# Attention denominators from GpSimd's sums of three P chunks, with the main and the dca denominator in one accumulation

## The reference, cut to what matters

```
y_dca  = y[:, -16:, :] ;  y_main = y[:, :-16, :]
q = LN(x @ Wq + bq) per head ;  k, v from y_main ;  k_dca, v_dca from y_dca
ctx     = softmax(q k^T * SCALE) v              # over 496 main rows
ctx_dca = softmax(q k_dca^T * SCALE) v_dca      # over 16 dca rows
x = x + (ctx + ctx_dca) @ Wo + bo
x = x + moe_ffn(layernorm(x))                   # 7 routed experts, top 2, and a shared one
```

## Time and profile before

| | us |
|---|---|
| median of three runs | 1215.59 |
| the profiled execution | 1215.54 |
| its span | 1213.4 |
| attention, first score matmul to last GpSimd instruction | about 188.0 to 512.3 |
| one group of four heads, in the middle of attention | 18.67 |

### The profile page before, as it was taken

The page is one execution under the profiler, slowest core; times in us unless marked ns, Lnnn a source line. Parts: engine busy times, 40 slices in busy tenths (PEclk is TensorE's granted clock), DMA queues, the critical chain, the costliest instruction groups (busy, mean ns, idle before and its releaser), DMA issues. The chain is left out here.

```text
span 1213.4 us, 18924 instructions
## 1 busy us (share of the span) xinstructions
PE 1050.7 (87%) x5825; PEld 478.9 (39%) x5826; DVE 631.5 (52%) x1123; ACT 491.9 (41%) x886; POOL 558.6 (46%) x505
## 2 busy tenths in 40 slices
PE   2789955999999999689439999999999999967896
PEld 1445431222222222145315545445545455523453
DVE  6777744677777777445543333233333322215644
ACT  2466553566666666323213333333333333312231
POOL 1365551143434421232337799898999800032111
PEclk9889985899999999889759999999999999989899
DMA  6144451222122211045136434333434311146244
GB/s 233 40 116 127 135 143 52 58 77 76 61 80 62 76 62 42 19 160 180 72 119 245 165 124 137 121 121 121 138 122 137 104 52 52 35 146 228 87 122 139
DMA packets 88074, 133.02 MB, mean 110 GB/s; under 512 B 7992, under 2 KB 46904, under 8 KB 88016
## 3 DMA queue, kind: packets, MB, share of 16 engines
q1 hardware_dynamic: 75040, 90.55, 23.5%
q0 software_dynamic: 11648, 40.38, 9.8%
q10 hardware_dynamic: 1328, 1.36, 0.4%
HBM read 85.60 MB, written 46.66 MB: 109 GB/s over the span
## 5 line engine op out<-in xcount | busy, mean ns | idle before, releaser
L866 DVE TENSOR_REDUCE nm<-a_psS 128x2 bf16<-128x992 f32 x128 | 152.8, 1194 | 83.9 <-PE a_psS L877 83.9
L807 ACT ACTIVATE p_t<-a_psT 128x512 f32<-128x512 f32 x256 | 145.6, 595 | 62.9 <-PE a_psT L893 59.0
L1706 PE MATMUL e_psU<-w_exp,e_xT 128*128 (+1 forms) x528 | 130.8, 384 | 11.4 <-issue 8.0
L1706 PE MATMUL e_psY<-w_exp,e_gT 128*128 (+1 forms) x528 | 128.1, 379 | 2.7 <-issue 1.7
L1706 PE MATMUL e_psG<-w_exp,e_uT 128*128 (+1 forms) x528 | 128.4, 379 | 2.2 <-DVE e_uT L1658 2.2
L893 PE MATMUL a_psT<-q_stk,k_stk 98*128 98x512 f16 x256 | 101.6, 402 | 0.4 <-ACT p_t L807 0.4
L877 PE MATMUL a_psS<-k_stk,q_stk 96*128 96x512 f16 x256 | 82.3, 405 | 21.9 <-DMA k_stk<-k_dram 14.5
L1687 DVE TENSOR_TENSOR e_g<-e_g,e_u 128x512 f32<-128x512 f32 x44 | 51.6, 1172 | 91.6 <-ACT e_g L1623 91.6
L175 POOL TENSOR_TENSOR w_exp<-e_raw,w_exp 128x1024 f32 (+1 forms) x42 | 90.8, 2161 | 6.0 <-POOL e_raw L172 4.5
L1658 DVE TENSOR_TENSOR e_gT<-e_psGT,e_gT 128x512 f16<-128x512 f32 x44 | 30.4, 692 | 108.0 <-ACT e_gT L1596 108.0
L900 PE MATMUL a_psD<-p_t,ones 128*32 128x512 f32 x640 | 85.1, 607 | 0.0
(11 more groups left out here) (315 smaller groups left out, 1875.1 us busy)
## 6 DMA issues: line engine op xcount, KB each, us to landing
e_x<-xs_dram SPq DMA_DIRECT2D x38, 256.0 KB, 2.8
ys_dram<-e_y SPq DMA_DIRECT2D x38, 256.0 KB, 2.0
q_dram<-q_st SPq DMA_DIRECT2D x24, 256.0 KB, 2.8
k_dram<-k_st SPq DMA_DIRECT2D x24, 256.0 KB, 3.6
q_stk<-q_dram SPq DMA_DIRECT2D x64, 96.0 KB
k_stk<-k_dram SPq DMA_DIRECT2D x64, 96.0 KB
e_raw<-in_L_ffn_Wup_dram POOLq DMA_DIRECT2D x12, 512.0 KB, 4.2
e_raw<-in_L_ffn_Wgate_dram POOLq DMA_DIRECT2D x12, 512.0 KB, 4.2
```

The source lines that it names most:

```text
L807: act.activation(probs(w, k), psT[:, k % 2], ACT.Exp, scale=SCALE / (QS * QS)).then_inc(s["exp"], 1)
L866: dve.tensor_reduce(pair[:, :, 0:1].rearrange("p q o -> p (q o)"), psS[:, :, 0:NMAIN], AX.X, ALU.max, negate=True)
L1706: ins = pe.matmul(dst[:, :], stationary, moving, start=(k == 0 and chunks[0] == 0), stop=(k == len(terms) - 1 and chunks[-1] == KD - 1))
```

## The change

The sum of the chunks 0, 1 and 2 of P is formed by POOL in fp32 (`p_sums`, two additions of 128 x 512 for each head, into a ring `p_sum` of six slots). The denominators then take two pieces of PE in place of five: ones by `p_sum`, and a mask by chunk 3. The mask has 32 columns: the first 16 take the main rows, the last 16 the dca rows, and the stationary of ones has zeros in its last 16 columns. So one accumulation holds both denominators, in different rows of each strip. DVE transposes it once, inverts both with one reciprocal, and transposes back twice. The order of the pieces on PE changes, as do the halves in which DVE, ACT and POOL do the final steps. The rings of P chunks shrink from (6, 7, 7, 8) to (5, 5, 6, 7), and ACT also waits for the sums before it reuses a slot. The split of the early weights is as it was.

```diff
-            pool.memset(ones[:, 0, :], 1.0).then_inc(s["masks"], 1)
+            pool.memset(ones[:, 0, 0:HD // 2], 1.0)
+            pool.memset(ones[:, 0, HD // 2:HD], 0.0).then_inc(s["masks"], 1)
...
-            dve.tensor_copy(ones[:, 1, :], m_main[:, :].broadcast_to([P, HD]))
-            dve.tensor_copy(ones[:, 2, :], m_dca[:, :].broadcast_to([P, HD]))
+            dve.tensor_copy(ones[:, 1, 0:HD // 2], m_main[:, :].broadcast_to([P, HD // 2]))
+            dve.tensor_copy(ones[:, 1, HD // 2:HD], m_dca[:, :].broadcast_to([P, HD // 2]))
...
-    RING = (6, 7, 7, 8)
+    RING = (5, 5, 6, 7)
+    SUMS = 6
...
-    d_t = sb("d_t", [P, S], F32)
-    d_rec = sb("d_rec", [P, S // HD, 1], F32)
+    p_sum = sb("p_sum", [P, SUMS, S], F32)
+    d_rec = sb("d_rec", [P, S // HD, 2], F32)
...
+            def p_sums(w):
+                at_least(pool, s["sums_mm"], (w - SUMS) // G + 1)
+                t_ = p_sum[:, w % SUMS, :]
+                pool.wait_ge(s["exp"], TB * w + 2)
+                pool.tensor_tensor(t_, probs(w, 0), probs(w, 1), ALU.add).then_inc(s["sum_1"], 1)
+                pool.wait_ge(s["exp"], TB * w + 3)
+                pool.wait_ge(s["sum_1"], w + 1)
+                pool.tensor_tensor(t_, t_, probs(w, 2), ALU.add).then_inc(s["sum_2"], 1)
             for u in range(LAST):
                 gr, h = group(u, 0)
-                if there(gr - 1) and h == 4:
+                if head(u - 2):
+                    p_sums(u - 2)
+                if there(gr - 1) and h == 2:
                     pool.wait_ge(s["o_main"], gr)
                     pool.wait_ge(s["o_dca"], gr)
                     pool.tensor_tensor(o_sum[:, :], o_sum[:, :], r_dca[:, :], ALU.add).then_inc(s["o_sum"], 1)
-                if there(gr - 1) and h == 6:
+                if there(gr - 1) and h == 4:
...
                 if w >= RING[k]:
                     act.wait_ge(s["v_mm"], TB * ((w - RING[k]) // G) + k + 1)
+                    if k < TB - 1:
+                        act.wait_ge(s["sum_2"], w - RING[k] + 1)
+                    else:
+                        act.wait_ge(s["dca_mm"], (w - RING[k]) // G + 1)
                 act.activation(probs(w, k), psT[:, k % 2], ACT.Exp, scale=SCALE / (QS * QS)).then_inc(s["exp"], 1)
 
             def hi_part(gr, h):
-                if there(gr - 1) and h == 4:
+                if there(gr - 1) and h == 3:
                     b, c = divmod(gr - 1, KD)
                     act.wait_ge(s["o_sum"], gr)
...
-            def main_part(gr, h):
+            def blocks(x):
+                return x.rearrange("p (a o) -> p a o", o=HD)
+            def spread(which):
+                return d_rec[:, :, which:which + 1].broadcast_to([P, S // HD, HD])
+            def inverse(gr, h):
                 if there(gr) and h == 4:
                     dve.wait_ge(s["d_mm"], gr + 1)
-                    dve.transpose(d_t[:, :], psD[:, :]).then_inc(s["d_seen"], 1)
+                    at_least(dve, s["o_main"], gr)
+                    dve.transpose(r_main[:, :], psD[:, :]).then_inc(s["d_seen"], 1)
                 if there(gr) and h == 5:
                     dve.wait_ge(s["d_seen"], gr + 1)
-                    dve.reciprocal(d_rec[:, :, :], d_t[:, :].rearrange("p (a o) -> p a o", o=HD)[:, :, 0:1]).then_inc(s["d_rec"], 1)
+                    at_least(dve, s["rec_dca"], gr)
+                    dve.reciprocal(d_rec[:, :, :], blocks(r_main[:, :])[:, :, 0:HD // 2 + 1:HD // 2]).then_inc(s["d_rec"], 1)
                 if there(gr) and h == 6:
                     dve.wait_ge(s["d_rec"], gr + 1)
-                    dve.transpose(r_main[:, :].rearrange("p (a o) -> p a o", o=HD), d_rec[:, :, :].broadcast_to([P, S // HD, HD])).then_inc(s["rec_main"], 1)
+                    dve.transpose(blocks(r_main[:, :]), spread(0)).then_inc(s["rec_main"], 1)
+                if there(gr) and h == 7:
+                    at_least(dve, s["o_sum"], gr)
+                    dve.transpose(blocks(r_dca[:, :]), spread(1)).then_inc(s["rec_dca"], 1)
+                    dve.wait_ge(s["v_mm"], TB * (gr + 1))
+                    dve.wait_ge(s["rec_main"], gr + 1)
+                    at_least(dve, s["o_lo"], gr)
+                    dve.tensor_tensor(o_sum[:, :], psO[:, :], r_main[:, :], ALU.mult).then_inc(s["o_main"], 1)
                 if there(gr - 1) and h == 0:
-                    dve.wait_ge(s["v_mm"], TB * gr)
-                    dve.wait_ge(s["rec_main"], gr)
-                    at_least(dve, s["o_lo"], gr - 1)
-                    dve.tensor_tensor(o_sum[:, :], psO[:, :], r_main[:, :], ALU.mult).then_inc(s["o_main"], 1)
-            def dca_part(gr, h):
-                if there(gr) and h == 7:
-                    dve.wait_ge(s["dca_mm"], gr + 1)
-                    dve.transpose(d_t[:, :], psD[:, :]).then_inc(s["dd_seen"], 1)
-                if there(gr - 1) and h == 0:
-                    dve.wait_ge(s["dd_seen"], gr)
-                    dve.reciprocal(d_rec[:, :, :], d_t[:, :].rearrange("p (a o) -> p a o", o=HD)[:, :, 0:1]).then_inc(s["dd_rec"], 1)
-                if there(gr - 1) and h == 1:
-                    dve.wait_ge(s["dd_rec"], gr)
-                    at_least(dve, s["o_sum"], gr - 1)
-                    dve.transpose(r_dca[:, :].rearrange("p (a o) -> p a o", o=HD), d_rec[:, :, :].broadcast_to([P, S // HD, HD])).then_inc(s["rec_dca"], 1)
-                if there(gr - 1) and h == 2:
+                    dve.wait_ge(s["dca_mm"], gr)
                     dve.wait_ge(s["rec_dca"], gr)
                     dve.tensor_tensor(r_dca[:, :], psOd[:, :], r_dca[:, :], ALU.mult).then_inc(s["o_dca"], 1)
...
-            def four(dst, stationary, gr, k, first, last):
+            def four(dst, stationary, gr, moving, first, last):
                 for j in range(G):
                     n = gr * G + j
-                    ins = pe.matmul(dst[j * HD:(j + 1) * HD, :], stationary(n), probs(n, k), start=first, stop=last, tile_position=(0, j * HD))
+                    ins = pe.matmul(dst[j * HD:(j + 1) * HD, :], stationary(n), moving(n), start=first, stop=last, tile_position=(0, j * HD))
                 return ins
-            def denominator(gr, k):
-                if k == 0:
-                    at_least(pe, s["dd_seen"], gr)
-                pe.wait_ge(s["exp"], TB * (gr * G + G - 1) + k + 1)
-                ins = four(psD, lambda n: ones[:, 1 if k == TB - 1 else 0, :], gr, k, k == 0, k == TB - 1)
-                if k == TB - 1:
-                    ins.then_inc(s["d_mm"], 1)
+            def denominators(gr, last):
+                if not last:
+                    at_least(pe, s["d_seen"], gr)
+                    pe.wait_ge(s["sum_2"], (gr + 1) * G)
+                    four(psD, lambda n: ones[:, 0, :], gr, lambda n: p_sum[:, n % SUMS, :], True, False).then_inc(s["sums_mm"], 1)
+                else:
+                    four(psD, lambda n: ones[:, 1, :], gr, lambda n: probs(n, TB - 1), False, True).then_inc(s["d_mm"], 1)
             def values(gr, k):
                 if k == 0:
                     at_least(pe, s["o_main"], gr)
-                four(psO, lambda n: v_all[:, k, n, :], gr, k, k == 0, k == TB - 1).then_inc(s["v_mm"], 1)
+                pe.wait_ge(s["exp"], TB * (gr * G + G - 1) + k + 1)
+                four(psO, lambda n: v_all[:, k, n, :], gr, lambda n: probs(n, k), k == 0, k == TB - 1).then_inc(s["v_mm"], 1)
             def dca(gr):
                 at_least(pe, s["o_dca"], gr)
-                four(psOd, lambda n: v_all[:, TB, n, :], gr, TB - 1, True, True)
-                pe.wait_ge(s["d_seen"], gr + 1)
-                four(psD, lambda n: ones[:, 2, :], gr, TB - 1, True, True).then_inc(s["dca_mm"], 1)
+                four(psOd, lambda n: v_all[:, TB, n, :], gr, lambda n: probs(n, TB - 1), True, True).then_inc(s["dca_mm"], 1)
             def chunk(gr, h):
-                if h < TB:
-                    denominator(gr, h)
-                if TB - 1 <= h < 2 * TB - 2:
-                    values(gr, h - TB + 1)
-                if h == 2 * TB - 2:
+                if h in (0, 1):
+                    values(gr, h)
+                if h in (2, 3):
+                    if h == 3:
+                        pe.wait_ge(s["exp"], TB * (gr * G + G))
+                    denominators(gr, h == 3)
+                if h in (4, 5):
+                    values(gr, h - 2)
+                if h == 6:
                     dca(gr)
-                if h == 2 * TB - 1:
-                    values(gr, TB - 1)
```

More of the change, by code:

```diff
@@ L117, in build @@
         O_BYTES = B * KD * 2 * S * 2
-        CONST = 2848 + 256 + 3 * HD * 4
+        CONST = 2848 + 256 + 2 * HD * 4
         const = Map(nc, SBUF_HI - CONST, SBUF_HI)
@@ L121, in build @@
         ident_b = const("ident_b", [P, P], BF16)
-        ones = const("ones", [P, 3, HD], F32)
+        ones = const("ones", [P, 2, HD], F32)
         m_main = const("m_main", [P, 1], F32)
@@ L719, in attend @@
     o_sum = sb("o_sum", [P, S], F32)
```

(5 more changed lines are left out.)

## The result

| | before | changed |
|---|---|---|
| median, runs on the same chip | 1216.9 us | 1228.44 us |
| lowest and highest of the five runs | 1213.75, 1219.01 | 1225.23, 1232.39 |
| the profiled execution | 1215.54 | 1227.31 |
| its span | 1213.4 | 1225.6 |
| end of attention (last L794 before, last L808 after, start + duration) | 512.3 | 523.5 |

The change is slower: the ratio of the times is 1.0093, with a 95% interval of 1.0065 to 1.0120. Of the 12.2 us that the span grew, 11.2 are there when attention ends. The intervals of all ratios come from several executions; each length of 14 periods is that of one profiled execution.

What follows compares the result with a forecast made beforehand. PE's second pieces and a DVE loop bounded the kernel before; afterwards POOL's loop with ACT, 20.2 us a group, would. Periods +15.6, start -0.9 and end -4.3 gave +10.4, that is 1226 us, range 1203 to 1239.

Steps and rivals of the forecast that it cites:

- The limit on PE: In attention before the change, only the two of ten PE pieces second in their half set time, 0.87 us each.
- the sum of halves: A group's period before the change, added from its halves: 4 x 2.17 + 4 x 2.06 + 2 x 0.87 = 18.66 us.
- POOL's loop: While weights are split, POOL's work 17.9, waits 0.5 and idle time with ACT 1.8 make a group 20.2 us.
- ACT's hold without load: ACT's late rounding of o_sum holds PE 1.0 us a group, making 18.4 us without POOL's load.
- PE and DVE alone: A group of the changed kernel by PE and DVE only: 17.4 us, keys taken at nothing.
- the hold covers late keys: PE's 2.8 us hold covers operands issued late by SP, which otherwise would show as up to 1.4 us a group.
- The sum: Over attention: 14 periods +15.6 us, the start -0.9, the end -4.3, together +10.4 us.
- I expect no fall: PE's granted clock stays at 1.00 despite a pause of some 2.8 us in each group.
- the 26 of the bound: If PE's clock fell, a tenth of the 261 us between transposes could add up to 26; within a 12% rival.
- PE's wait: PE waits about 2.8 us in each group, at a_psT, for ACT's exponential behind the rounding.
- The signs: From 260 to 440 us: POOL busy 89%, transpose periods near 20.2 us, ACT idle 2 us or more, PE 80%, clock 1.00.
- A lock between DVE and POOL: POOL standing behind DVE's transposes and reciprocal: loop up to 1.65 us longer, +18, 1244 us; within a 12% rival.

Runs made afterwards that it cites:

- e6: Kernel before, without the denominator pieces of chunks 1 and 2, each the only piece of its half; ratio 1.0014, 14 periods 266.06 us.
- e10: Kernel before, without two pieces second in their half (chunk 3's denominator, the dca denominator); ratio 0.9871, 14 periods 245.89 us.
- e1: Changed kernel with ACT's rounding moved one half later, from h = 3 to h = 4; ratio to the kernel before 0.9911, 14 periods 255.20 us.
- e5: Changed kernel with one more addition on POOL in each group; ratio to the kernel before 1.0254, 14 periods 296.24 us.
- e2: Changed kernel with POOL's weight split replaced by small additions, rounding kept at h = 3; ratio to the kernel before 0.9885, 14 periods 252.19 us.
- e3: Changed kernel without POOL's weight split and with the rounding at h = 4; ratio to the kernel before 0.9842, 14 periods 248.89 us.
- e4: Changed kernel with one more PE piece, chunk 3's values done twice in h = 5; ratio to the kernel before 1.0144, 14 periods 281.51 us.
- e8: Changed kernel with the rounding at h = 4 and the split's high part made by ACT; ratio to the kernel before 0.9883, 14 periods 252.67 us.
- e11: As e8, with DVE's two final multiplications one half later, five operand slots for four, five sum slots for six; ratio to the kernel before 0.9818, 1196.53 us.

## Why the prediction was right

The forecast was 1226.0 us, from a sum of +10.4; measured were 1228.44 us, or +11.5 between the medians. Point by point:

- **The limit on PE**: as read. PE lost 30% of its pieces, and of its pieces those that are second in a half have a price, single ones next to none (e6 against e10). The price was taken too high, 0.87 us a piece against 0.55 in e10; it had been chosen so that the sum of halves closes, not read from a row.
- **POOL's loop**: forecast 17.9 + 0.5 + 1.8 = 20.2 us, measured 20.05. The addition was 1.27 us (took 1.275), the idle time ahead of L792 1.78 (took 1.8). That the loop is the cause is shown by e1 and e5.
- **ACT's hold without load**: forecast a period of 18.4, measured 18.0 to 18.1. The hold was 0.2 to 0.8 us (e2) rather than 1.0.
- **PE and DVE alone**: forecast 17.4, measured 17.8 (e3). That the hold covers late keys was right: PE waits for keys 0.3 us in 180 us of the changed kernel, and 9.7 us in e1, which has no hold, about 1.0 a group where the forecast had up to 1.4. The 17.4 itself had keys at nothing, and in e3 they cost 0.57.
- **The sum**: periods +15.7 (forecast +15.6), the start -0.7 (-0.9), from the last transpose to the last POOL instruction -3.8 (-4.3), together +11.2 in attention, against the +10.4 of the sum. The end of the stage is the same chain as in the earlier trace rows:

```profile
520.36 1.26 POOL L804 TENSOR_TENSOR o_sum<-o_sum,r_dca 128x512 f32<-128x512 f32 x1 [2.75 <-DVE r_dca L874]
522.36 1.15 POOL L808 TENSOR_TENSOR oT_all<-o_sum,oT_all 128x512 f16<-128x512 f32 x1 [0.74 <-ACT oT_all L831]
```

- **"I expect no fall"**: this step failed. The clock fell, and two periods of L804 were longer for it, by 1.2 and 1.0 us. That is 2.2 us, not the 26 of the bound: POOL, not PE, set the pace, and PE at half speed mostly used up time in which it would have waited. The waits show it: 1.0 to 1.4 us in the turn behind a fall, 2.5 to 3.0 in the others, and the L804 periods that hold the falls of 265 to 275 and 310 to 315 us (0.83 over 10 us, both) are 20.03 and 20.04 us as ever. The 0.3 us of the period of 20.34 lie elsewhere: its clock was 1.00, and a second addition of POOL waited longer than usual for the first. The row is shown behind this list. The sum of the periods came out within 0.1 us by luck: against these 2.5 us stand a loop shorter by 0.15 (11 x 0.15 = 1.7), and an entry into it and an exit from it that were shorter by 0.4 and 0.3. Without that luck the time would have been some 2.4 us further from the forecast, still well inside its range.
- **PE's wait**: forecast 2.8 us a group, measured 23.7 us in the nine groups of 260 to 440 us, 0.4 of each group's 2.6 in `h = 7`. So 2.2 on average, about what is left of 20.05 above the 17.8 of e3.
- **The signs**: POOL was busy for 86% of 260 to 440 us (forecast 89%), PE for 83% (80%), and ACT waited 3.6 us a group for `o_sum` (2 or more). The periods of DVE's transpose were 20.3 only on average, and the clock was 0.94 there and not 1.00.
- **A lock between DVE and POOL**: none seen. POOL's additions take 1.268 and 1.269 us on average with DVE's transposes beside them. The Trainium skill (GPSIMD Engine Reference, Elementwise — side-by-side cycle accounting) has some 2.6 cycles per element for such an addition, by which it would be 1.11 us, an estimate; the 128 additions of this kernel stand 14% above that.

The row behind the period of 20.34 us:

```profile
305.05 1.26 POOL L795 TENSOR_TENSOR p_sum<-p_sum,p_t 128x512 f32<-128x512 f32 x1 [0.45 <-POOL p_sum L792]
```

Its cause is open; e1 and e4 have the same row once, with 0.44 us.

## What to carry to other kernels

Before giving work to an engine that seems half idle, add up two things: its work for a period, and the time in which it must stand idle in a loop with engines that run their lists in order. Here 10.2 + 7.7 us of work would have fitted (e1), but a rounding that stood half a step too early let ACT wait for POOL and then POOL for ACT, and turned a gain of 0.9% into a loss of 0.9%. And what taking a piece from the busiest engine brings depends on its place: find by arithmetic which pieces close the period before counting any as gained.

## What the runs showed of the hardware

PE's clock fell where I expected none. In the changed kernel the granted clock of 385 to 390 us was 0.86 and of the 5 us behind it 0.50. PE had been busy for 2.19 us of the first, with one pause of 2.81:

```profile
345.00:350.00 5.00, 2.38 (x21) 0.85 (x24) 1.69 (x4) 2.28 (x5) 3.08 (x3) 1.00 0.41 143
385.00:390.00 5.00, 2.19 (x15) 0.72 (x10) 1.29 (x3) 2.19 (x5) 3.08 (x4) 0.86 0.38 137
390.00:395.00 5.00, 5.00 (x18) 0.84 (x20) 2.79 (x4) 2.25 (x4) 4.86 (x4) 0.50 0.12 30
...
388.93 0.61 PE L910 MATMUL a_psT<-q_stk,k_stk 98*128 98x512 f16 x1 [2.81 <-ACT p_t L825]
```

But the very similar stretch of 345 to 350 us, with 2.38 us busy and a pause of 2.62, kept 1.00, and in e6 the clock fell behind a pause of 1.37 us, and again behind pauses of 0.53 us at most (300 to 310 us, 0.66), while a stretch of the same kind at 320 to 325 us kept 1.00. The kernels with the longest pauses of PE from 260 to 440 us (3.0 us in the changed one, 2.3 in e4, 3.0 in e5) had mean clocks of 0.94 to 0.96 from 250 to 470 us. In e1, e2, e3 and e8 to e11 none was over 1.6 us, and the clock was 1.00; but e11 had one of 1.4 us, as long as the longest of e6, whose mean was 0.97. So the longest pauses go with falls, but a fall needs none, and what decides in a single case is left open. One consequence is seen in the profiled execution of e6: a kernel with pieces taken from PE can have longer periods, when its lighter stretches are followed by a lower clock and PE is the limit. And what a fall costs depends on the limit: two of the four falls of the changed kernel cost nothing, as PE's next wait was 1.0 to 1.4 us in place of 2.5 or more, and the two deeper ones cost 1.2 and 1.0 us.
